# Mamba scan: three of sixteen inflows per chunk as TensorE products, every odd C product on GpSimd; last experts: the first two Silu built from Exp and Ln

## The chip, the cores and the metric

The kernel runs on one NeuronCore of a Trainium2 chip. The metric is the device time of one execution in microseconds. A core has TensorE (PE, matrix products into PSUM), VectorE (DVE), ScalarE (ACT), GpSimd (POOL) and SyncE (SP, which issues the transfers here). They run side by side, each through its own list of instructions in order, and wait for one another on semaphores.

## The reference, cut to what matters

Eight layers of a network over 2048 tokens with 128 channels, each `x = x + layernorm(layer(layernorm(x)))`. The change touches the last two.

```python
# layer 6, Mamba: 256 inner channels d, 16 states n
dA = jnp.exp(d_i[..., None] * A)                          # decay
h  = dA * h + (d_i * u_i)[..., None] * B_i[:, None, :]    # inflow: (delta*x) times B of the token
y  = jnp.einsum('bdn,bn->bd', h, C_i)
# layer 7, mixture of experts
h1 = jnp.einsum('td,eid->tei', xf, w1); h3 = jnp.einsum('td,eid->tei', xf, w3)
h  = jax.nn.silu(h1) * h3
y  = jnp.einsum('tei,edi,te->td', h, w2, comb)
```

## The kernel before

The sequence is cut into CHUNKS = 4 chunks of N = 512 tokens. Channels lie on the 128 partitions, in two halves i = 0, 1; tokens run along the free axis. The scan is 64 steps, one for each chunk c and state n (step = 16c + n). A step is made of these pieces:

- **Decays.** ScalarE writes exp(A·delta), one 128x512 half at a time, into one of three PSUM banks that take turns (`state_step`, `decays`).
- **Inflow.** GpSimd multiplies delta·x (`g[:, 6:8]`, both halves, 128x1024) by the row B_n, which SyncE has loaded into all partitions from DRAM (`b_times_du`, `b_copy`; four places, four steps ahead).
- **Scan.** VectorE runs two `tensor_tensor_scan`, one for each half (`scan`), into one of four state buffers: `g` for steps 0 and 1 of four, `y` for 2 and 3.
- **C product.** The states times the row C_n. VectorE reads the row from the one PSUM bank C_BANK (`times_c`), where TensorE has spread it over the partitions (`spread_c`, the `g,sel` product). For the steps in `BY_POOL` GpSimd does it with a row loaded from DRAM (`states_times_c`). The result lies in `tmp` or `rstd`.
- **Sum over n.** TensorE adds the products to PSUM banks 0 and 1 with an identity (`sum_n`, two 128x512 products; these are the `tmp,const` and `rstd,const` rows). Every float32 product shows as two matmul records in the trace, a bfloat16 one as one.

At n = 3 of the next chunk VectorE multiplies the two finished banks by the gate (`gate`, the row `g<-ps,g` 128x1024). Until that is done `sum_n` of the next chunk's first step may not start, since it clears the same banks. Then TensorE makes the output product (`out_of`, the `g,arena` rows), and the norms around layer 7 follow at n = 6, 8, 10, 12 and 14 (`post6_...`, `pre7_...`, `add_back6`, `h_back7`, `router7`).

All orders are written out by hand: each engine has a loop over the steps with `if`s for what is put between them. On VectorE the loop at k holds the extras of n = k mod 16, then `scan(k + 1)`, then `times_c(k)` unless k is in BY_POOL. On TensorE the loop at `step` holds `sum_n(step - 3)` for a step of GpSimd, `sum_n(step - 2)` for one of VectorE, the extras, and `spread_c(step + 1)` if that step is VectorE's.

After the scan come layer 7's turns, in each of which one pair of experts meets one chunk (`gate_up7`, `silu`, `glu7`, `hidden_hi`, `down7`). Routing for the first two chunks (`group_scores7`, `group_order7`, `kept7`, `chosen7`) is done on VectorE meanwhile. ScalarE has one table set for Exp and Ln and another for Silu, and loads a table when the set changes.

Of the kernel before, what the change touches and what calls it, by code (L numbers as in the profile page):

```python
# [29 lines left out]
P = 128  # L30
T = 2048
N = 512
# [66 lines left out]
BY_POOL = [s for s in range(STEPS) if s % 16 in (1, 3, 6, 8, 11, 13)]  # L99
# [147 lines left out]
def sandwich(nc, x, out, weights, bools, moe0, moe1, consts, selectors, rope):  # L247
    ctx = ExitStack()
    with ctx:
        def sb(name, shape, dt=F32):  # L250
# [12 lines left out]
            hid_ready e_done rows_stored row_loaded0 row_loaded1 a_ready xs_bank xs_ready conv_ready  # L263
            xa_ready z_bank z_ready dt_bank dt_ready dl_ready du_ready bc_bank bc_step dt_clipped bcp_ready b_copied
            cb_bank da_ready db_ready hs_done hc_ready hc_pool c_loaded0 c_loaded1 sum_done carry_saved
# [164 lines left out]
        def decays(step, i):  # L430

            return ps[:, DA_BANKS[(2 * step + i) % 3], :]
# [4 lines left out]
        def b_copy(step):  # L437
            home = arena[0][:, 1792:3840] if step < 48 else g[:, 8, :]
            return home[:, step % 4 * N:(step % 4 + 1) * N]
# [17 lines left out]
        def by_dve(step):  # L457
            return step + 1 - by_pool(step)

# [4 lines left out]
        def _(sp):  # L464
# [6 lines left out]
            for layer in range(LAYERS):  # L471
# [29 lines left out]
                if layer == 6:  # L501
# [14 lines left out]
                    for step in range(STEPS):  # L516
                        k = step % 4
# [7 lines left out]
                        if step == 48:  # L525
                            sp.wait_ge(s["dl_ready"], 2 * CHUNKS)
                        if step >= 4:
                            sp.wait_ge(s["db_ready"], step - 3)
                        sp.dma_start(b_copy(step), bc_dram[step % 16:step % 16 + 1, cols(step // 16)].to_broadcast([P, N]))\
                          .then_inc(s[f"row_loaded{k}"], 16)  # L530
                        if step - 7 in BY_POOL[:-2]:
                            load_c(by_pool(step - 7) + 1)
                if layer == 7:
# [6 lines left out]
                    for half in range(2):  # L540
# [4 lines left out]
                        for r in range(1, 9):  # L545
                            use = 8 * half + r - 1
                            if use < 4:
                                sp.wait_ge(s[f"row_loaded{use}"], ROWS_BEFORE[use] + 256)
# [79 lines left out]
        def _(pe):  # L628
# [594 lines left out]
            def xs(c):  # L1223
                h(6, c)
                for i in range(2):
                    mm(ps[:, 4 * i + c, :], W(6, "wx", i * 128, i * 128 + 128), H(c)).then_inc(s["xs_bank"], 1)
# [13 lines left out]
            for c in range(CHUNKS):  # L1240
                pe.wait_ge(s["xs_ready"], 2 * c + 2)
                for i in range(2):
                    mm(ps[:, 4 * i + c, :], W(6, "wz", i * 128, i * 128 + 128), H(c)).then_inc(s["z_bank"], 1)
            for c in range(CHUNKS):
                pe.wait_ge(s["z_ready"], 2 * c + 2)
                pe.wait_ge(s["xa_ready"], 2 * c + 2)
# [2136 lines left out]
```

## Time and profile before

| | us |
|---|---|
| median of 3 runs | 1102.28 (1101.16 to 1107.06) |
| the profiled execution, its time | 1102.07 |
| its span in the trace | 1100.1 |
| scan, from its first to its last step | 767.8 to 983 |
| busy over the span: TensorE / VectorE / GpSimd / ScalarE | 932.5 / 822.2 / 679.1 / 602.8 |

The time is 2.0 us more than the span. Busy shares of the span mix stages with different limits, so what matters for this change is read from the stretch of the scan and the 30 us after it. PE rows are products, PEld rows weight loads. `x4` after a row is the number of records in it. The bracket at its end is how long the engine had been idle and what it had waited for. Records of one engine can overlap by some 0.1 us at their ends, so the pace of a series is the distance from start to start.

### The profile page before, as it was taken

How to read it: one execution, taken by the hardware profiler on the slowest of the kernel's cores; microseconds unless marked ns; L12 is line 12 of the kernel's file. 1: busy time of each engine (PE TensorE's matmuls, PEld its weight loads, DVE VectorE, ACT ScalarE, POOL GpSimd, SP SyncE). 2: the span in 40 equal slices, each digit the busy share in tenths (PEclk: the TensorE clock that was granted, in tenths of full speed). 3: DMA queues.
4: the chain of work that ended last, by engine and by line, in shares of the span. 5: the costliest groups of instructions: out<-in, count | busy, mean ns of one | idle time of the engine just before them, and what ended most of it. 6: DMA issues, size and time to landing. Idle time of an engine off the chain costs nothing.

```text
span 1100.1 us, 11087 instructions
## 1 busy us (share of the span) xinstructions
PE 932.5 (85%) x2909; PEld 547.9 (50%) x2909; DVE 822.2 (75%) x1163; ACT 602.8 (55%) x1095; POOL 679.1 (62%) x469
## 2 busy tenths in 40 slices
PE   6869976688889957899999999987577787887997
PEld 3324432233337725688888888732223333335775
DVE  4895437999965568666666666587999999986755
ACT  5756675300356754455565555686444545545556
POOL 3030134699852133577777777619999999962773
PEclk9989998699999968899999999998788988897999
DMA  2000120000020004377666667302334334424251
GB/s 82 1 0 1 50 77 18 0 0 1 0 71 1 11 19 101 94 157 152 138 151 153 148 141 156 90 0 76 106 108 113 113 103 114 106 72 105 70 145 39
DMA packets 33449, 84.68 MB, mean 77 GB/s; under 512 B 4352, under 2 KB 14208, under 8 KB 29216
## 3 DMA queue, kind: packets, MB, share of 16 engines
q1 hardware_dynamic: 33408, 84.20, 30.5%
q8 instruction: 17, 0.28, 0.1%
q14 instruction: 24, 0.20, 0.1%
HBM read 82.22 MB, written 1.97 MB: 77 GB/s over the span
## 4 chain that ended last, share of the span: by engine, by line
PE 36%; DVE 16%; ACT 3%; issue 3%; POOL 1%; DVEq 0%; ACTq 0%; POOLq 0%
PE ps L630 35%; DVE y L3167 5%; DVE g L3167 5%; DVE tmp L2468 1%; DVE g L2468 1%; DVE rstd L2468 1%; ACT rstd L1440 1%; DVE ps L2468 1%; POOL g L2424 1%; ACT g L1440 1%; ACT ps L1440 1%; DVE normed L2468 0%; ACT sq L1440 0%; ACT parts L1440 0%; DVE g L3123 0%
## 5 line engine op out<-in xcount | busy, mean ns | idle before, releaser
L630 PE MATMUL ps<-parts 128*128 128x512 f32 x1704 | 416.5, 403 | 17.5 <-DVE g L2468 6.2
L630 PEld LDWEIGHTS ps<-parts 128*128 128x128 f32 x1704 | 321.6, 190 | 107.1 <-issue 18.3
L630 PE MATMUL ps<-g,arena 128*128 128x512 f32 (+2 forms) x408 | 191.2, 608 | 26.6 <-POOL g L2351 15.1
L1440 ACT ACTIVATE g<-ps 128x512 f32<-128x512 f32 (+1 forms) x216 | 127.3, 596 | 147.5 <-PE ps L630 143.1
L2302 POOL TENSOR_TENSOR parts<-g,parts 128x512 fp32r<-128x512 f32 x112 | 144.4, 1290 | 60.8 <-ACT parts L1440 57.9
L2468 DVE TENSOR_TENSOR ps<-g,ps 128x512 f32<-128x512 f32 x160 | 111.3, 695 | 94.5 <-PE ps L630 72.8
L1440 ACT ACTIVATE ps<-g,small 128x512 f32<-128x512 f32 x131 | 89.8, 688 | 98.3 <-DVE y L3167 52.9
L630 PEld LDWEIGHTS ps<-g,arena 128*128 128x128 f32 (+1 forms) x408 | 76.9, 197 | 133.1 <-issue 88.9
L1440 ACT ACTIVATE parts<-g 128x512 fp32r<-128x512 f32 (+3 forms) x243 | 125.9, 547 | 24.7 <-DVE g L2468 17.6
L2424 POOL TENSOR_TENSOR g<-g,arena 128x1024 f32<-128x1024 f32 x48 | 113.7, 2396 | 0.1
L2468 DVE TENSOR_TENSOR g<-ps,g 128x512 f32<-128x512 f32 (+1 forms) x140 | 98.9, 706 | 18.1 <-DVE ps L2468 3.3
L2292 POOL TENSOR_TENSOR parts<-g,parts 128x512 fp32r<-128x512 f32 x56 | 72.4, 1295 | 64.0 <-ACT parts L1440 63.8
L630 PE MATMUL ps<-normed,arena 128*128 128x512 f32 x136 | 76.0, 667 | 21.2 <-DVE g L2468 8.2
L2351 POOL TENSOR_TENSOR g<-g 128x1024 f32<-128x1024 f32 x32 | 76.2, 2391 | 19.5 <-DVE g L2826 18.5
L630 PE MATMUL ps<-tmp,const 128*128 128x512 f32 x128 | 73.3, 709 | 9.6 <-DVE g L2468 9.6
L3167 DVE TENSOR_TENSOR_SCAN g<-ps,carry,g 128x512 f32<-128x512 f32 x64 | 77.6, 1260 | 0.9 <-ACT ps L1440 0.9
L3167 DVE TENSOR_TENSOR_SCAN y<-ps,carry,g 128x512 f32<-128x512 f32 x64 | 77.8, 1261 | 0.0
L2826 DVE TENSOR_TENSOR_SCAN g<-ps,g 128x512 f32<-128x512 f32 x64 | 76.7, 1245 | 0.0
L1440 ACT ACTIVATE rstd<-ps,small 128x512 f32<-128x512 f32 x68 | 46.6, 685 | 38.5 <-PE ps L630 38.2
L630 PE MATMUL ps<-rstd,const 128*128 128x512 f32 x128 | 65.3, 640 | 0.0
L1440 ACT ACTIVATE sq<-ps 128x512 f32<-128x512 f32 x28 | 16.5, 593 | 87.8 <-PE ps L630 87.8
L630 PE MATMUL ps<-sq,const 128*128 128x512 f32 x96 | 52.5, 636 | 8.1 <-ACT sq L1440 5.9
(226 smaller groups left out, 1182.2 us busy)
## 6 DMA issues: line engine op xcount, KB each, us to landing
g<-coef_scratch SPq DMA_DIRECT2D x56, 512.0 KB, 6.2
arena<-bc_scratch SPq DMA_DIRECT2D x48, 256.0 KB, 3.3
g<-in_moe_dram SPq DMA_DIRECT2D x34, 192.0 KB, 4.7
g<-coef_scratch SPq DMA_DIRECT2D x24, 256.0 KB, 5.5
sq<-bc_scratch SPq DMA_DIRECT2D x24, 256.0 KB, 3.3
arena<-coef_scratch SPq DMA_DIRECT2D x24, 256.0 KB, 4.3
g<-bc_scratch SPq DMA_DIRECT2D x16, 256.0 KB, 3.3
g<-in_rope_dram SPq DMA_DIRECT2D x1, 2048.0 KB, 8.7
```

Source lines behind the costliest of these rows:

```text
L630: return nc.tensor.matmul(o, lhsT, rhs, start=start, stop=stop, **kw)
L1440: return nc.scalar.activation(o, i, func, **kw)
L2292: pv.tensor_tensor(hid_lo[:, cols(n % 4)], hidden, hid_hi[:, cols(n % 4)].bitcast(F32), ALU.subtract).then_inc(s["hl_ready"], 1)
L2302: pv.tensor_tensor(hid_lo[:, cols(c)], g[:, 6, (c % 2) * N:(c % 2 + 1) * N], hid_hi[:, cols(c)].bitcast(F32), ALU.subtract).then_inc(s["hl ...
L2351: pv.tensor_tensor(g[:, 2, 2 * par * N:(2 * par + 2) * N].rearrange("p (r n) -> p r n", r=2), fast_states(e), g[:, 8:10, cols(c)], ALU.mul ...
L2424: pv.tensor_tensor(inflow(step), g[:, 6:8, cols(step // 16)], b_copy(step).unsqueeze(1).to_broadcast([P, 2, N]), ALU.mult).then_inc(s["db_ ...
L2468: return v.tensor_tensor(o, a, b, op)
L2826: last = v.tensor_tensor_scan(state, fast_decay(c), two_of(0, 11, k)[:, r, :], state[:, N - 1:N] if c else 0.0, ALU.mult, ALU.add)
L3167: ins = v.tensor_tensor_scan(states(step % 4)[:, i, :], decays(step, i), inflow(step)[:, i, :], carry[:, n + 16 * i:n + 16 * i + 1], ALU.m ...
```

## The change

Three things change.

1. In steps with n = 6, 10 and 14 (`BY_PE`, 12 of 64) the inflow is a TensorE product: delta·x turned so that tokens are on partitions (`du_turned`) times a 128x128 diagonal of B's values (`b_diag`), four 128x128 products for each half, into the PSUM bank that the decays had. The decays of these steps go to the SBUF place that the inflow had. For this TensorE turns B (`b_turned`) and delta·x (`du_into`, `du_turn`), and ScalarE copies what was turned (`du_copied`) and builds the diagonals (`diag_of_b`, four 128x128 instructions a step).
2. `BY_POOL` becomes every odd step but the last: 31 steps in place of 24.
3. In layer 7 the first two Silu are x·exp(-ln(1 + exp(-x))), with a clip and two multiplications on VectorE (`clip_gate7`, `glu7`) and three functions on ScalarE (`sigmoid_of`), so that they run before the Silu table is loaded. Turn 2's gate and up products, and both routing steps `kept7` and `chosen7`, move forward.

```diff
-BY_POOL = [s for s in range(STEPS) if s % 16 in (1, 3, 6, 8, 11, 13)]
+BY_POOL = [s for s in range(STEPS - 1) if s % 2 == 1]
+BY_PE = [s for s in range(STEPS) if s % 16 in (6, 10, 14)]
+B_ROWS = [s for s in range(STEPS) if s not in BY_PE]
...
         def decays(step, i):
-            return ps[:, DA_BANKS[(2 * step + i) % 3], :]
+            return inflow(step)[:, i, :] if step in BY_PE else flow_bank(step, i)
+        def flow(step, i):
+            return flow_bank(step, i) if step in BY_PE else inflow(step)[:, i, :]
...
+            def b_turned():
+                for c in range(CHUNKS):
+                    for a in range(TILES):
+                        at = 256 + (c * TILES + a) * 16
+                        last = mm(ps[:, 0, at:at + 16], bc_whole[:, c * N + a * P:c * N + (a + 1) * P], ident[0:96, 0:16])
+                last.then_inc(s["dut_bank"], 1)
+            def du_into(bank, c, half):
+                for a in (2 * half, 2 * half + 1):
+                    for i in range(2):
+                        at = (a % 2 * 2 + i) * P
+                        last = nc.tensor.transpose(ps[:, bank, at:at + P], g[:, 6 + i, c * N + a * P:c * N + (a + 1) * P],
+                                                   ident)
+                last.then_inc(s["dut_bank"], 1)
...
+            def inflow_by_pe(step):
+                c = step // 16
+                pe.wait_ge(s["x_parts"], diag_parts(step))
+                for i in range(2):
+                    pe.wait_ge(s["hs_done"], 2 * step + i - 2)
+                    for a in range(TILES):
+                        last = mm(flow(step, i)[:, a * P:(a + 1) * P], du_turned(c, a, i),
+                                  b_diag(step)[:, a * P:(a + 1) * P])
+                    last.then_inc(s["x_bank"], 1)
...
             spread_c(0)
+            b_turned()
+            pe.wait_ge(s["du_ready"], 1)
+            du_into(4, 0, 0)
+            du_into(7, 0, 1)
...
             for step in range(STEPS):
                 c, n = step // 16 - 1, step % 16
+                if step + 1 in BY_PE:
+                    inflow_by_pe(step + 1)
                 if step - 3 in BY_POOL:
                     sum_n(step - 3)
...
+                if c < 2 and n in (11, 15):
+                    du_turn(c + 2, n // 15)
                 if step + 1 < STEPS and step + 1 not in BY_POOL:
                     spread_c(step + 1)
...
-            pre7_var(3)
             coef_turned7(0)
             coef_turned7(1)
+            pre7_var(3)
+            gate_up7(2)
             router7(3)
...
             for step in range(STEPS):
                 c, n = step // 16 - 1, step % 16
                 state_step(step)
                 if step == 1:
+                    act.wait_ge(s["dut_bank"], 1)
+                    f(b_by_token, ps[:, 0, 256:512], ACT.Copy).then_inc(s["x_parts"], 1)
+                    du_copied(0, 0)
+                    du_copied(0, 1)
...
                 if step >= 2:
                     save_carry(step - 2)
+                if step + 3 in BY_PE:
+                    diag_of_b(step + 3)
...
+            sigmoid_of(0)
             post6_square(3)
             post6_root(3)
-            pre7_square(3)
-            pre7_root(3)
+            sigmoid_of(1)
             coef_copied7(0)
             coef_copied7(1)
+            pre7_square(3)
+            hidden_hi(0)
+            pre7_root(3)
             sigmoid7(1)
...
-                        if step + 4 < STEPS:
+                        if step + 4 in B_ROWS:
                             b_times_du(step + 4)
...
             h_back7(2)
+            group_scores7(0)
             gate(CHUNKS - 1)
+            clip_gate7(0)
+            group_order7(0)
             clip7(2)
-            group_scores7(0)
-            group_order7(0)
             kept7(0)
+            chosen7(0)
+            clip_gate7(1)
+            glu7(0)
             add_back6(3)
-            chosen7(0)
+            glu7(1)
             h_back7(3)
```

**TensorE's list after a gate.** These are the instructions from `spread_c(18)` on in the program before, up to the second C row that is spread after the gate; the product that waits for `yg_ready` is `sum_n(16)`, the first behind the gate.

```order
L630 MATMUL ps<-g,sel 128x512 [waits hc_ready]
L630 MATMUL ps<-tmp,const 128x512 [waits hc_ready,yg_ready]
L630 MATMUL ps<-tmp,const 128x512
L630 MATMUL ps<-g,arena 128x512 [waits yg_ready]
L630 MATMUL ps<-g,arena 128x512
L630 MATMUL ps<-g,sel 128x512 [waits hc_ready]
L630 MATMUL ps<-tmp,const 128x512 [waits hc_pool]
L630 MATMUL ps<-tmp,const 128x512
L630 MATMUL ps<-rstd,const 128x512 [waits hc_ready]
L630 MATMUL ps<-rstd,const 128x512
L630 MATMUL ps<-g,sel 128x512 [waits hc_ready]
```

The same place in the changed program, from `sum_n(15)` on.

```order
L663 MATMUL ps<-rstd,const 128x512 [waits hc_pool]
L663 MATMUL ps<-rstd,const 128x512
L663 MATMUL ps<-tmp,const 128x512 [waits hc_ready,yg_ready]
L663 MATMUL ps<-tmp,const 128x512
L663 MATMUL ps<-g,arena 128x512 [waits x_parts,yg_ready]
L663 MATMUL ps<-g,arena 128x512
L663 MATMUL ps<-g,sel 128x512 [waits hc_ready]
L663 MATMUL ps<-tmp,const 128x512 [waits hc_pool]
L663 MATMUL ps<-tmp,const 128x512
L663 MATMUL ps<-rstd,const 128x512 [waits hc_ready]
L663 MATMUL ps<-rstd,const 128x512
L663 MATMUL ps<-arena,g 128x128 [waits hs_done,x_parts]
```

The row `arena,g` is the first of the eight products of step 22's inflow. It stands behind `sum_n(16)`, `out_of(0)`, `spread_c(20)`, `sum_n(17)` and `sum_n(18)`.

**ScalarE's list at the start of the scan.** The rows `ps<-g,small` are the decays; those that follow the copies belong to step 2. Before:

```order
L1440 ACTIVATE ps<-g,small 128x512 [waits hs_done]
L1440 ACTIVATE arena<-ps 128x256 [waits setup_bank]
L1440 ACTIVATE ps<-g,small 128x512 [waits hs_done] x2
L1440 ACTIVATE carry<-g 128x2 [waits hs_done]
```

In the changed program:

```order
L1521 ACTIVATE ps<-g,small 128x512 [waits hs_done]
L1521 ACTIVATE arena<-ps 128x256 [waits dut_bank]
L1521 ACTIVATE g<-ps 128x512 [waits dut_bank] x2
L1521 ACTIVATE arena<-ps 128x256 [waits setup_bank]
L1521 ACTIVATE ps<-g,small 128x512 [waits hs_done] x2
L1521 ACTIVATE carry<-g 128x2 [waits hs_done]
```

Three copies that wait for TensorE (`dut_bank`: B turned, then the two halves of delta·x turned) now stand ahead of step 2's decays.

## Rows read from the trace of the kernel before

**Rows 1.** Windows: length, busy (count) PE, PEld, DVE, ACT, POOL; clock; DMA; GB/s.
```profile
767.80:983.00 215.20, 161.64 (x346) 67.86 (x345) 210.98 (x183) 107.51 (x216) 208.50 (x91) 0.86 0.39 108
```

**Rows 2.** Groups of instructions on VectorE, 767.8 to 983: busy, mean ns, idle before.
```profile
L2468 DVE TENSOR_TENSOR tmp<-g,ps 128x1024 f32<-128x1024 f32 x20 | 23.9, 1197 | 3.1 <-PE ps L630 2.9
```

**Rows 3.** Groups of instructions on GpSimd, 767.8 to 983.
```profile
L2424 POOL TENSOR_TENSOR g<-g,arena 128x1024 f32<-128x1024 f32 x47 | 111.4, 2397 | 0.0
...
L2434 POOL TENSOR_TENSOR tmp<-g,sq 128x1024 f32<-128x1024 f32 x12 | 29.2, 2437 | 3.0 <-PE ps L630 2.0 <-DVE g L3167 1.0
```

**Rows 4.** Waits, 767.8 to 983: total, times, longest.
```profile
DVE tmp L2468 <- PE ps L630: 2.9, 2, 1.9
...
DVE rstd L2468 <- PE ps L630: 0.6, 1, 0.6
```

**Rows 5.** Timeline at the first gate: VectorE, then TensorE.
```profile
834.42 1.19 DVE L2468 TENSOR_TENSOR rstd<-y,ps 128x1024 f32<-128x1024 f32 x1
835.53 1.21 DVE L2468 TENSOR_TENSOR g<-ps,g 128x1024 f32<-128x1024 f32 x1
836.67 4.79 DVE L3167 TENSOR_TENSOR_SCAN g<-ps,carry,g 128x512 f32<-128x512 f32 x4
843.39 1.22 DVE L2468 TENSOR_TENSOR tmp<-g,ps 128x1024 f32<-128x1024 f32 x1 [1.94 <-PE ps L630]
...
836.80 3.78 PE L630 MATMUL ps<-tmp,const 128*128 128x512 f32 x4 [4.61 <-DVE g L2468]
840.37 2.77 PE L630 MATMUL ps<-g,arena 128*128 128x512 f32 x4
842.97 0.38 PE L630 MATMUL ps<-g,sel 96*128 96x512 bf16 x1
```

**Rows 6.** Timeline of TensorE at the second gate, which ends at 891.74.
```profile
891.79 1.98 PE L630 MATMUL ps<-tmp,const 128*128 128x512 f32 x4 [2.45 <-DVE g L2468]
893.61 1.88 PE L630 MATMUL ps<-g,arena 128*128 128x512 f32 x4
895.33 0.38 PE L630 MATMUL ps<-g,sel 96*128 96x512 bf16 x1
```

**Rows 7.** Timeline of TensorE at the third gate, which ends at 943.83.
```profile
943.89 3.18 PE L630 MATMUL ps<-tmp,const 128*128 128x512 f32 x4 [2.55 <-DVE g L2468]
...
949.12 0.38 PE L630 MATMUL ps<-g,sel 96*128 96x512 bf16 x1
```

**Rows 8.** A window of 4 us, TensorE only: length, busy (count), clock, DMA, GB/s.
```profile
836.00:840.00 4.00, 3.20 (x4) 0.50 0.49 118
```

**Rows 9.** Timeline at the start of the scan.
```profile
767.03 1.22 PE L630 MATMUL ps<-const,arena 128*128 128x128 f32 x4 [6.67 <-DVE g L3139]
...
771.50 0.69 ACT L1440 ACTIVATE ps<-g,small 128x512 f32<-128x512 f32 x1 [0.48 <-DVE g L3167]
...
773.67 2.45 DVE L3167 TENSOR_TENSOR_SCAN y<-ps,carry,g 128x512 f32<-128x512 f32 x2
```

**Rows 10.** Timeline of TensorE: small products, first a router, then transposes.
```profile
989.97 0.96 PE L630 MATMUL ps<-arena,normed 128*128 128x16 f32 x8
...
1092.59 1.04 PE L1430 MATMUL ps<-const,normed 128*128 128x128 f32 x8
```

**Rows 11.** Timeline behind the scan.
```profile
990.96 0.23 DVE L3057 TENSOR_SCALAR g<-ps 128x64 f32<-128x64 f32 x1 [2.87 <-PE ps L630]
...
994.54 0.70 DVE L2468 TENSOR_TENSOR ps<-ps,sq 128x512 f32<-128x512 f32 x1
...
997.35 0.29 DVE L3098 SCALAR_TENSOR_TENSOR arena<-arena,g 128x128 f32<-128x128 f32 x1
...
1000.88 1.89 PE L630 MATMUL ps<-arena,normed 128*128 128x16 f32 x8 [0.42 <-DVE normed L2468]
...
1004.17 1.28 ACT L1440 ACT_TABLE_LOAD   x1
...
1009.31 0.70 DVE L2468 TENSOR_TENSOR ps<-g,ps 128x512 f32<-128x512 f32 x1 [1.40 <-PE ps L630]
```

More of the change, by code:

```diff
@@ L458, in by_dve, with by_pe, of_rows, turned_parts @@
             return step + 1 - by_pool(step)
+        def by_pe(step):
+            return sum(k <= step for k in BY_PE)
+        def of_rows(step):
+            return step + 1 - by_pe(step)
+        def turned_parts(c, part):
+            return 1 + part if c == 0 else 3 + 5 * (c - 1) + 3 + part
+        def diag_parts(step):
+            return 3 + 5 * (step // 16) + BY_PE.index(step) % 3 + 1
         block = ctx.enter_context(nc.Block())
@@ L524, in _ @@
                             sp.wait_ge(s["rows_stored"], 96)
[L525 to L532, printed above, removed]
+                        if step not in BY_PE:
+                            use = of_rows(step) - 1
+                            if use >= 4:
+                                sp.wait_ge(s["db_ready"], use - 3)
+                            sp.dma_start(b_copy(use), bc_dram[step % 16:step % 16 + 1, cols(step // 16)]
+                                         .to_broadcast([P, N])).then_inc(s[f"row_loaded{use % 4}"], 16)
+                        if step - 6 in BY_POOL[:-2]:
+                            load_c(by_pool(step - 6) + 1)
                 if layer == 7:
@@ L2025, in state_step, with du_copied, diag_of_b @@
                       scale=neg_a[:, n + 16 * i:n + 16 * i + 1]).then_inc(s["da_ready"], 1)
+            def du_copied(c, half):
+                act.wait_ge(s["dut_bank"], 2 * c + half + 2)
+                at = c % 2 * 1024 + half * N
+                f(g[:, 8, at:at + N], ps[:, 7 if (c, half) == (0, 1) else 4, :], ACT.Copy).then_inc(s["x_parts"], 1)
+            def diag_of_b(step):
+                act.wait_ge(s["x_parts"], 1)
+                if by_pe(step) > 2:
+                    act.wait_ge(s["x_bank"], 2 * (by_pe(step) - 2))
+                for a in range(TILES):
+                    at = (step // 16 * TILES + a) * 16 + step % 16
+                    last = f(b_diag(step)[:, a * P:(a + 1) * P], ident, ACT.Copy, scale=b_by_token[:, at:at + 1])
+                last.then_inc(s["x_parts"], 1)
             def save_carry(step):
@@ L3159, in scan @@
                 n = step % 16
-                dve.wait_ge(s["db_ready"], step + 1)
+                if step not in BY_PE:
+                    dve.wait_ge(s["db_ready"], of_rows(step))
                 if step >= 4:
```

104 lines of the change are left out of this document (72 added, 32 removed).

## The prediction

> **What bounds the kernel now.** I read the windows first, since only the scan and the start of layer 7 change. In the scan's 215.2 us VectorE is busy for 211.0 and GpSimd for 208.5, TensorE for 162 and ScalarE for 108 [rows 1]. So VectorE sets the end of the scan with 4.2 us of idle time, GpSimd is close behind, and both have to shrink for the scan to. The groups give the price of what moves: a C product takes VectorE 1.20 us [rows 2] and GpSimd 2.44, and an inflow takes GpSimd 2.40 [rows 3]. VectorE's idle time is mostly waiting for TensorE [rows 4]: 1.9 and 1.0 us ahead of C products into `tmp` and 0.6 ahead of one into `rstd`. The longest is behind a gate: the C product at 843.39 came 1.94 us late [rows 5].
>
> **How a gate works.** The gate ends at 836.74. The four scans behind it take from 836.67 to 841.46 [rows 5], so I count 2.4 us for the two scans of a step, and 1.11 us for a C product (834.42 to 835.53). TensorE had been idle for 4.61 us, because `sum_n(16)` may not clear the banks before the gate has read them, and restarted at 1.2 GHz: its granted clock from 836 to 840 was 0.50 [rows 5, 8]. The sum took 3.57 us from start to start, `out_of` 2.60, and the next C row came at 842.97, 6.2 us behind the gate. At the second gate TensorE had been idle for 2.45 us and went on at twice that pace, 2.4 GHz: 1.82 us for the sum, 1.72 for `out_of`, and the C row 3.6 us behind the gate [rows 6]. At the third, after 2.55 us idle, the sum took most of 3.18 us and the C row came 5.3 us behind the gate [rows 7].
>
> **What is taken away.** Seven C products leave VectorE: 7 x 1.11 = 7.8 us. GpSimd loses 12 inflows and gains 7 C products, 5 fewer of about 2.4 us, so 12 us less. A chunk of 16 steps then costs VectorE 16 x 2.4 + 8 x 1.11 = 47.3 us and the extras (gate, add-back and norm, some 3.5), GpSimd 13 + 8 = 21 instructions or 50.4 us. VectorE with its 50.8 stays ahead by a hair, and a wait of VectorE's behind each gate gives GpSimd room. I take all 7.8; the bound below is GpSimd in front, which would eat up to 2.
>
> **What a TensorE inflow costs.** No row shows this product. The nearest are 128x128 transposes, 8 in 1.04 us or 0.12 apiece, and products of 16 columns, 8 records in 0.96 us, also 0.12 [rows 10], so the weight load of one seems to lie under the product of the other. A float32 product is two records. A step is 8 products, 16 records; at 0.11 us, half a step (4 products) is 0.86 us and the step 1.75. The other bound is load and product one after the other, twice that. I take the low one, as both rows are at it. The Trainium skill, TensorE: Matmul & The Clock Gate, Back-to-back issue gap, gives about 81 ns for each pass of 128 columns in a sustained stream with weight loads. By an estimate with four passes for a float32 product half a step would be 1.3 us, and the three gates together 1.3 us dearer than by the rows.
>
> **In the middle of a chunk** the rows say that it fits. Two steps of VectorE are 4 x 1.2 + 1.11 = 5.9 us. TensorE's work between the C product that lets it go on and the first half of an inflow is one C row (0.22), two sums (3.44) and 0.86, and with 0.15 of latency 4.7 us: 1.2 us early. At 1.2 GHz the same list is 0.43 + 7.1 + 1.72 + 0.15 = 9.4 us, 3.5 late. In chunk 0 VectorE's three long products (`g<-g`, 128x1024) leave TensorE idle between bursts, so I put 1.0 us on steps 6 and 10 together.
>
> **Behind a gate** it does not fit. The order shows that step 22's inflow stands behind `sum_n(16)`, which waits for the gate, then `out_of(0)`, `spread_c(20)`, `sum_n(17)` and `sum_n(18)`. VectorE wants it two steps and a C product behind the gate, at 5.9 us. At the full clock TensorE has 4 x 1.72 + 0.22 + 0.86 + 0.2 = 8.2: 2.3 us late. With the C row 6.2 us behind, as at the first gate, it is 6.2 + 0.22 + 3.44 + 0.86 + 0.15 = 10.9, or 5.0 late; with the third gate's 5.3, 4.1 late [rows 5 to 7]. Which clock? In the changed kernel `sum_n(15)` is done 1.95 us behind the C product of step 16, and the gate ends 7.1 behind it (four scans 4.8, a C product 1.1, the gate 1.2). TensorE is then idle for 5.2 us, longer than at the first gate, which came out at 1.2 GHz; of two waits of about 2.5 us one did. So I take 4.2 us a gate, near the two at 1.2 GHz: 12.6 for three, with 7 and 15 as ends. The waits for TensorE before (2.9 and 0.6, in all 3.5 [rows 4]; the timeline has all three within 8 us of a gate) are contained in it and come off.
>
> The Trainium skill, TensorE: Matmul & The Clock Gate, HAM oscillation, warns that repeated waits between bursts put the array back to half rate each time. By that rule all three gates would be at 1.2 GHz, at 13 to 15 us; one of three at the full clock is what this trace has against it.
>
> **At the start.** Step 2's decays were issued at 771.50, and its scan at 773.67 [rows 9]. Now three ScalarE copies stand ahead of them and wait for TensorE: 16 products that turn B (32 records) and 8 transposes. TensorE is free for them at about 768.5 (the group from 767.03 and one C row). At 0.12 us the records take 3.8, at 1.2 GHz 0.236 (the router at 1000.88, 1.89 for 8 [rows 11]) 7.6. I take a third of them at 1.2 GHz, 5.3 us, so 773.8; the transposes end at 774.7, the last copy at 775.4, the output weights' copy 775.8, the decays 776.5, and the scan starts at 776.55: 2.9 us late. Ends: 1.4 and 6.2. The later copies and diagonals lie in ScalarE's idle half; if that cover is gone, a diagonal group is 4 instructions of 0.3 to 0.4 us ahead of the next decays, which have 1.7 us to spare.
>
> **Behind the scan.** The path before: add-back at 994.54, router 1000.88, table load 1004.17, turn 2 on VectorE at 1009.31 [rows 11]. A VectorE product of 128x512 takes 0.70, so the add-back's two end at 995.94, and `chosen7` behind them takes the 1.7 us to 997.64. After the change a clip (0.7), `chosen7` and turn 0 (1.4) stand ahead of the add-back together with routing that was there before. VectorE's wait of 2.87 us for the router of chunk 2 is filled with the other clip and the routing's first part (1.9 in all), which leaves kept7 at 991.2. From there 1.6 + 1.7 + 0.7 + 1.4 put the add-back at 996.6, 2.1 late. The router of chunk 3, 6.3 us behind the add-back before, may start at 1002.9. It may also wait for turn 2's six products, which are put ahead of it. Router (1.0 or 1.9), clip and sigmoid (1.4), a weight copy (0.5), the table load (1.28) and turn 2's Silu (0.6): turn 2 starts on VectorE between 1007.6 and 1008.8. It had started at 1009.31, so 0.5 to 1.7 less; I take 1.1. Turns 0 and 1 are hidden in the routing's wait.
>
> **The sum** is made against the profiled execution's 1102.07, which is within 0.3 us of the median 1102.28: 1102.1 - 7.8 (C products) - 3.5 (the gates' old waits) + 12.6 (the gates' new ones) + 1.0 (chunk 0) + 2.9 (start) - 1.1 (turns) = **1106.2**, say 1106.
>
> **Rivals.**
> - *TensorE keeps the full clock.* The gates cost 2.3 each (6.9), the start 1.4 and chunk 0 nothing: 1102.1 - 7.8 - 3.5 + 6.9 + 1.4 - 1.1 = 1098. The second gate speaks for it [rows 6], and TensorE has about 20 us more to do, which keeps it awake; against it stands the 5.2 us of idling. Chance 0.22.
> - *No new wait behind the gates*, since the inflow comes in time by some slack I don't see (the sums faster, VectorE slower there). Only the start remains: 1102.1 - 7.8 - 3.5 + 2.9 - 1.1 = 1092.6. The list speaks against it: 1.72 four times alone is 6.9, over the 5.9. Chance 0.14.
> - *TensorE becomes the bound away from the gates too* (the slower side). The nine other inflows have 1.2 us to spare at the full clock and are 3.5 late at the lower. It decides as soon as TensorE has idled long enough ahead of one; in chunks 0 to 2 it idles for up to 3 us between bursts. Four of the nine at 1.2 GHz add 14, less the 1.0 that is counted: 1119. If instead load and product do not overlap, the gates cost 2.6 more and it is 1109. Together 0.16.
> - The forecast as it stands, 1101 to 1111: 0.48.
>
> **Range and chances.** 1092 to 1113 holds all but the far part of the third rival and the edge of the second; the forecast's own range is 1101 to 1111. A change under 0.5% (5.5 us) can't be told from none. Below 1096.8 lie the case without waits and a fifth of the full-clock one: 0.22. Above 1107.8 lie the third rival and a quarter of the forecast: 0.28. The rest, 0.50, is within 0.5%.
>
> **What the changed profile would show.** VectorE idle before a scan `y<-g,carry,ps` of steps 22, 38 and 54, released by TensorE, 2 to 5 us each; TensorE idle for about 5 us ahead of each gate; GpSimd with 52 inflows and 31 C products; VectorE's C products 33; step 2's scan about 3 us late with ScalarE's copies ahead of it; inflow products at 0.11 us a record; turn 2 near 1008. I am wrong if the scans behind the gates start on time, if waits show at steps 10 and 14 of a chunk, or if VectorE waits for GpSimd (`hc_pool` or `db_ready`) at all.

## The result: 1114.06 us, one per cent slower

The changed kernel takes 1114.06 us (median of 4 runs, 1113.91 to 1116.89) against 1103.32 before (4 runs beside it, 1101.16 to 1107.06): a recorded ratio of 1.009, 95% interval 1.0072 to 1.0108 (the plain quotient of the two medians is 1.0097). The forecast was 1106, in a range that ended at 1113. Its profiled execution took 1114.01, with a span of 1112.2.

The window answers to [rows 1], same length, columns as there:

```profile
767.80:983.00 215.20, 174.60 (x558) 92.11 (x559) 193.33 (x170) 118.37 (x263) 189.82 (x84) 0.86 0.43 97
```

VectorE's load fell, but it idles for 22 of the 215 us where it idled for 4. The view of waits (the changed kernel, 767.8 to 998: total, times, longest) says for whom, and answers to [rows 4]:

```profile
DVE y L3289 <- PE ps L663: 11.6, 5, 3.2
DVE y L3289 <- ACT ps L1521: 4.9, 1, 4.9
DVE tmp L2587 <- PE ps L663: 4.3, 3, 1.5
DVE g L3289 <- ACT ps L1521: 1.8, 2, 1.0
DVE rstd L2587 <- PE ps L663: 0.9, 1, 0.9
```

Nothing of GpSimd is in the list. Its groups from 767.8 to 998, in answer to [rows 3], have the 52 inflows and 31 C products of the forecast, at 2.36 us:

```profile
L2543 POOL TENSOR_TENSOR g<-g,arena 128x1024 f32<-128x1024 f32 x52 | 121.8, 2361 | 0.1
L2553 POOL TENSOR_TENSOR tmp<-g,sq 128x1024 f32<-128x1024 f32 x16 | 37.7, 2355 | 4.8 <-DVE g L3289 2.7 <-PE ps L663 2.0
L2553 POOL TENSOR_TENSOR rstd<-y,sq 128x1024 f32<-128x1024 f32 x15 | 35.4, 2359 | 22.7 <-DVE y L3289 19.3 <-PE ps L663 3.5
```

**The first gate**, timeline of VectorE and then of TensorE in the changed kernel, in answer to [rows 5]:

```profile
842.50 1.22 DVE L2587 TENSOR_TENSOR g<-ps,g 128x1024 f32<-128x1024 f32 x1
843.63 4.80 DVE L3289 TENSOR_TENSOR_SCAN g<-ps,carry,g 128x512 f32<-128x512 f32 x4
849.90 1.22 DVE L2587 TENSOR_TENSOR tmp<-g,ps 128x1024 f32<-128x1024 f32 x1 [1.47 <-PE ps L663]
854.32 2.45 DVE L3289 TENSOR_TENSOR_SCAN y<-g,carry,ps 128x512 f32<-128x512 f32 x2 [3.20 <-PE ps L663]
...
843.77 3.78 PE L663 MATMUL ps<-tmp,const 128*128 128x512 f32 x4 [4.01 <-DVE g L2587]
847.34 2.30 PE L663 MATMUL ps<-g,arena 128*128 128x512 f32 x4
849.48 0.38 PE L663 MATMUL ps<-g,sel 96*128 96x512 bf16 x1
849.70 1.88 PE L663 MATMUL ps<-tmp,const 128*128 128x512 f32 x4
851.41 1.88 PE L663 MATMUL ps<-rstd,const 128*128 128x512 f32 x4
853.13 1.95 PE L663 MATMUL ps<-arena,g 128*128 128x128 f32 x16
```

This is the list of the prediction. After 4.01 us of idling the sum takes 3.57 us from start to start, and the granted clock from 843 to 847 is 0.50, which is 1.2 GHz. Part of the output product is faster already (granted clock 0.85 from 847 to 851), and the C row stands 5.8 us behind the gate. Two sums of 1.72 and the first half of the inflow follow at 2.4 GHz. VectorE waits first for the C row, then for the inflow. The other two gates are the same to 0.1 us (1.43 and 3.20, 1.41 and 3.20), 13.9 in all. The first of the two waits depends on the execution: numbers 1 and 4 below, with the same list at the gates, have 0.96 to 1.40 there, and 3.20 each time for the inflow.

**The start**, ScalarE, TensorE and VectorE, in answer to [rows 9]:

```profile
778.09 0.39 ACT L1521 ACTIVATE arena<-ps 128x256 f32<-128x256 f32 x1 [5.51 <-PE ps L663]
...
771.20 6.85 PE L663 MATMUL ps<-const,arena 96*128 96x16 f32 x32
777.89 1.95 PE L1312 MATMUL ps<-const,g 128*128 128x128 f32 x8
...
781.43 2.46 DVE L3289 TENSOR_TENSOR_SCAN y<-ps,carry,g 128x512 f32<-128x512 f32 x2 [4.95 <-ACT ps L1521]
```

The 32 records that turn B take 6.85 us, 0.21 each. The window around them has a granted clock of 0.50, so all of it ran at 1.2 GHz:

```profile
770.50:785.00 14.50, 13.36 (x49) 10.11 (x47) 9.49 (x8) 7.85 (x18) 13.79 (x6) 0.50 0.24 76
```

The kernel before has the same clock at this place. A window of it, TensorE only (length, busy, clock, DMA, GB/s):

```profile
774.00:776.00 2.00, 2.00 (x4) 0.50 0.32 86
```

**Behind the scan** VectorE's turn 2 starts at 1020.24, 22.9 us behind the end of the last C product; before it was 24.7 (1009.31 [rows 11] against 984.65).

### The profile page after: what moved, and what is told of

It is laid out like the page before. It is cut to its first block, busy times and chain, and to the rows that moved or that the text cites. A ratio compares the mean times of both kernels' runs of the same rounds, so it can differ in the third digit from the quotient of the medians.

```text
span 1112.2 us, 11662 instructions
## 1 busy us (share of the span) xinstructions
PE 958.4 (86%) x3158; PEld 577.8 (52%) x3158; DVE 817.6 (74%) x1160; ACT 620.8 (56%) x1156; POOL 665.6 (60%) x464
## 4 chain that ended last, share of the span: by engine, by line
PE 39%; DVE 12%; ACT 3%; issue 3%; POOL 1%; DMA 1%; DVEq 0%; SPq 0%; ACTq 0%; POOLq 0%
PE ps L663 38%; DVE y L3289 4%; DVE g L3289 3%; DVE g L2587 1%; DVE tmp L2587 1%; ACT g L1521 1%; ACT rstd L1521 1%; DVE rstd L2587 1%; DVE ps L2587 1%; DMA g<-in_moe_dram 1%; ACT ps L1521 1%; POOL parts L2410 0%; POOL tmp L2553 0%; ACT sq L1521 0%; DVE normed L2587 0%
## 5 line engine op out<-in xcount | busy, mean ns | idle before, releaser
L1521 ACT ACTIVATE g<-ps 128x512 f32<-128x512 f32 (+1 forms) x222 | 131.0, 596 | 149.3 <-PE ps L663 142.4
L2543 POOL TENSOR_TENSOR g<-g,arena 128x1024 f32<-128x1024 f32 x52 | 121.8, 2361 | 0.1
L1521 ACT ACTIVATE ps<-g,small 128x512 f32<-128x512 f32 x107 | 72.0, 685 | 78.0 <-DVE y L3289 46.7
L663 PE MATMUL ps<-tmp,const 128*128 128x512 f32 x128 | 70.5, 680 | 11.8 <-DVE g L2587 11.8
L663 PEld LDWEIGHTS ps<-normed,arena 128*128 128x128 f32 x136 | 27.6, 210 | 60.9 <-issue 44.9
```

Source lines behind the costliest of these rows:

```text
L663: return nc.tensor.matmul(o, lhsT, rhs, start=start, stop=stop, **kw)
L1521: return nc.scalar.activation(o, i, func, **kw)
L2543: pv.tensor_tensor(inflow(step), g[:, 6:8, cols(step // 16)], b_copy(use).unsqueeze(1).to_broadcast([P, 2, N]), ALU.mult).then_inc(s["db_r ...
```

## The experiments

Each was timed against the kernel before on the same chip (medians there 1104.51 for the first four, then 1103.15, then 1103.69). The ratios are the recorded ones; they can differ by 0.001 from the quotient of the medians. "Scan" is from the start of the first scan to the end of the last C product, "behind" from there to the end of the span, both from the profiled execution.

| kernel | median us | ratio to before | 95% | scan | behind |
|---|---|---|---|---|---|
| before | 1103.32 | 1 | | 216.8 | 115.5 |
| changed | 1114.06 | 1.0090 | 1.0072 to 1.0108 | 226.8 | 114.9 |
| 1 copies later | 1109.67 | 1.0055 | 1.0036 to 1.0073 | 221.4 | 114.8 |
| 2 inflow first | 1108.99 | 1.0041 | 1.0028 to 1.0054 | 222.7 | 114.8 |
| 3 TensorE kept busy | 1107.01 | 1.0031 | 1.0017 to 1.0045 | 220.7 | 115.2 |
| 4 scan only | 1114.31 | 1.0073 | 1.0044 to 1.0101 | 227.5 | 112.8 |
| 5 turns only | 1102.41 | 0.9986 | 0.9964 to 1.0007 | 216.6 | 115.0 |
| 6 two inflows | 1105.19 | 1.0022 | 0.9996 to 1.0049 | 219.2 | 115.5 |
| 7 GpSimd odd, no inflows | 1118.60 | 1.0133 | 1.0106 to 1.0160 | 232.8 | 114.1 |
| 8 two inflows, mended | 1102.40 | 0.9983 | 0.9966 to 1.0000 | 217.8 | 113.8 |
| 9 and weights earlier | 1096.53 | 0.9936 | 0.9916 to 0.9955 | 210.5 | 112.8 |
| 10 and third inflow at step 8 | 1094.85 | 0.9921 | 0.9899 to 0.9943 | 208.1 | 114.3 |
| 11 and the new turns | 1096.39 | 0.9926 | 0.9898 to 0.9953 | 209.0 | 114.8 |
| 12 changed, weights earlier | 1111.69 | 1.0077 | 1.0052 to 1.0101 | 225.7 | 115.6 |

**1. ScalarE's copies one step later.** They stand behind the decays of step 2 now.

```diff
                 state_step(step)
-                if step == 1:
+                if step == 2:
                     act.wait_ge(s["dut_bank"], 1)
                     f(b_by_token, ps[:, 0, 256:512], ACT.Copy).then_inc(s["x_parts"], 1)
```

> ScalarE's three start copies stand behind step 2's decays instead of ahead of them; nothing else differs from the changed kernel (1114). If the copies in ScalarE's list cause the 4.95 us ahead of step 2's scan, that wait goes to under 1 us and the time to 1109 to 1111. Rival: TensorE's turning of B and delta-x itself is what is late, so the wait only moves, to the C product of step 2 or to step 6's inflow, and the time stays at 1113 to 1115.

The wait of 4.95 us before step 2 is gone. One of 0.78 us before step 3 is left, and in chunk 0 step 10 waits 2.02 us where steps 6 and 10 had waited 1.37 and 0.59. The scan is 5.4 us shorter, and the median 4.4. So TensorE's slow turning of B costs 4.95 us only because ScalarE's copies stand ahead of step 2's decays; one step later it costs little.

**2. The gate's inflow ahead of the two sums.** Step 22's inflow (and 38's, 54's) is issued one step earlier in TensorE's order.

```diff
-                if step + 1 in BY_PE:
+                if step + 1 in BY_PE and not (step > 16 and (step + 1) % 16 == 6):
                     inflow_by_pe(step + 1)
+                if step > 16 and step % 16 == 4:
+                    inflow_by_pe(step + 2)
```

> Behind each gate the inflow products of n = 6 stand ahead of the sums of n = 1 and 2 in TensorE's list. If the place in the list is the cause, the 3.20 us ahead of the scans of steps 22, 38 and 54 go, the 1.4 us ahead of the C product at the gate stay, and the time is 1114 - 9.6 = 1104 to 1106. Rival: TensorE is simply full around the gates, so that the two sums pushed back make the next C row or inflow late by as much: 1111 to 1114.

VectorE behind the first gate of this kernel:

```profile
847.63 1.22 DVE L2589 TENSOR_TENSOR tmp<-g,ps 128x1024 f32<-128x1024 f32 x1 [0.99 <-PE ps L663]
848.77 2.44 DVE L3291 TENSOR_TENSOR_SCAN y<-g,carry,ps 128x512 f32<-128x512 f32 x2
...
858.74 0.70 DVE L2589 TENSOR_TENSOR ps<-ps,sq 128x512 f32<-128x512 f32 x1 [1.70 <-ACT sq L1523]
```

The three waits of 3.20 us are gone. In their place the add-back waits 1.70 us each time: the sums are later, the variance product behind them too, and ScalarE's root after it. Of 9.6 us, 5.1 are given back there, and the scan is 4.1 us shorter. The time, 1108.99, lies between the two that were expected: TensorE has a backlog behind a gate, and this order moves half of the cost to another wait.

**3. TensorE kept busy through the wait for the gate.** Four unread products stand ahead of the sum that waits.

```diff
+                if step > 16 and step % 16 == 2:
+                    if c:
+                        pe.wait_ge(s["sc_clipped"], 2 + c)
+                    for _ in range(4):
+                        mm(ps[:, 7, :], averaging, G(6, 0))
                 if step >= 2 and step - 2 not in BY_POOL:
                     sum_n(step - 2)
```

> Four products more, whose result nothing reads, stand between the sum of n = 15 and the first sum behind each gate, so that TensorE idles less than 2 us there; the output is unchanged. If the clock of 1.2 GHz behind the gate makes 4.7 us out of the 2.3 that the list alone costs, the granted clock behind the gates is 1.00, the wait ahead of the C product goes, the one ahead of the inflow falls to about 2.3, and the time is 1114 - 7 = 1106 to 1109. Rival: the clock does not follow these 3 us of work, the waits stay at 1.4 and 3.2, and the time at 1113 to 1115.

TensorE and VectorE at its first gate:

```profile
841.39 1.88 PE L663 MATMUL ps<-tmp,const 128*128 128x512 f32 x4
843.11 1.88 PE L663 MATMUL ps<-g,arena 128*128 128x512 f32 x4
844.83 0.38 PE L663 MATMUL ps<-g,sel 96*128 96x512 bf16 x1
...
849.67 2.45 DVE L3294 TENSOR_TENSOR_SCAN y<-g,carry,ps 128x512 f32<-128x512 f32 x2 [2.61 <-PE ps L663]
```

The sum takes 1.72 us instead of 3.57 (granted clock 1.00 from 840 to 852), the C row comes in time, and 2.61 us remain before the inflow. The prediction had 2.3 for a gate at the full clock. The scan is 6.1 us shorter, 2.0 a gate: that was the price of the clock, and the other 2.6 are TensorE's work.

**4. The changed scan with the old turns of layer 7.** The functions and the order behind the scan are those of before, for example

```diff
-            for n in range(2, len(TURNS7)):
-                if n > 2:
-                    gate_up7(n)
+            for n in range(2, len(TURNS7)):
+                gate_up7(n)
```

> The changed scan with the old first turns of layer 7 (Silu from its table, routing and turn 2 in their old places). The stretch behind the scan took 0.6 us less in the changed kernel than before, so this should take 0 to 1 us more than the changed kernel: 1114 to 1115. Rival: the changed turns lose time and the shorter stretch is the scan's doing; then this is 1112 or less.

The stretch behind the scan took 112.8 us, 2.1 less than with the new turns, as the rival had it; the median is that of the first expectation (1114.31 against 1114.06). The profiled execution, which is the median one, entered the scan 1.7 us later and took 0.7 more for it, so that the two readings do not contradict each other.

**5. The kernel before with the new turns.**

```diff
+            def clip_gate7(n):
+                dve.wait_ge(s["g_bank"], TURN7 + n + 1)
+                v.tensor_scalar(silu7(n), ps[:, 4 if n == 0 else 7, :], -80.0, None, ALU.max).then_inc(s["dt_clipped"], 1)
```

and the rest of the turns' edits as in the change. The clip is the first of the instructions from which the two Silu are built.

> The kernel before with one thing changed: the new first two turns of layer 7 (Silu from Exp and Ln, and the order around them); the scan is the old one. Theory 1, the prediction's term: the turns give 1.1 us back, 1103.4 against 1104.5 before. Theory 2, from the run with the scan alone changed (the stretch behind the scan took 112.8 us with the old turns and 114.85 with the new): the new turns cost 2 us wherever they stand, 1106.5. Theory 3: with the old scan the stretch behind it is one at 1.2 GHz in either order (three groups of small products at 1.9 to 2.1 us), so the turns make no difference, 1104.5 within 0.5. The trace is to tell 2 from 3: in 2 the second turn's first glu on VectorE stands 2 us later behind the scan than in the kernel before (24.7 us), in 3 it stands where it was.

0.9986, with 1 inside the interval: at most 4 us gained and at most 0.8 lost. Turn 2 starts 23.0 us behind the last C product (24.7 before), and yet the whole stretch shrinks by 0.5 only. Turn 2 is neither 2 us later (second theory) nor where it was (third). That does not show a gain by the turns either: in number 4, with the old turns, it starts at 22.9 too. The section on the prediction comes back to this.

**6. Two inflows a chunk on TensorE**, at steps 10 and 14; step 6's goes back to GpSimd. The two counters of copies (`turned_parts`, `diag_parts`) follow.

```diff
-BY_PE = [s for s in range(STEPS) if s % 16 in (6, 10, 14)]
+BY_PE = [s for s in range(STEPS) if s % 16 in (10, 14)]
```

> The changed kernel with two inflows a chunk on TensorE (steps 10 and 14) in place of three; step 6's goes back to GpSimd. Theory A (the waits at the gates are TensorE's backlog, and the inflow of step 6 is the last thing in it): the three waits of 3.20 us go, the waits of 1.4 us ahead of the C product stay, and chunk 0's step 6 loses its 1.4: 1114.1 - 9.6 - 1.4 = 1103, a scan of about 216. GpSimd has 4 instructions more, 87 at 2.36 = 205 us, and does not bind. Theory B (what leaves TensorE is given back elsewhere, as in the run with the inflow issued earlier): the add-back of each chunk waits 1.7 us instead, 1108. Theory C (GpSimd is already close to the bound, as a product with C at odd steps stands in a row with inflows): VectorE waits for GpSimd in every chunk, over 1112.

The 3.20s and chunk 0's 1.37 are gone, GpSimd holds nothing up, and the C products wait 2.14, 1.70 and 1.48. But a new wait stands near the end, on VectorE:

```profile
971.99 2.46 DVE L3289 TENSOR_TENSOR_SCAN g<-ps,carry,g 128x512 f32<-128x512 f32 x2 [3.94 <-ACT ps L1521]
985.16 1.22 DVE L2587 TENSOR_TENSOR rstd<-y,ps 128x1024 f32<-128x1024 f32 x1 [3.77 <-PE ps L663]
```

In the changed kernel the first was 0.98 and the second 0.89. Number 9 is on it.

**7. The kernel before with the C products of all odd steps on GpSimd** and no inflow on TensorE.

```diff
-BY_POOL = [s for s in range(STEPS) if s % 16 in (1, 3, 6, 8, 11, 13)]
+BY_POOL = [s for s in range(STEPS - 1) if s % 2 == 1]
...
-                        if step - 7 in BY_POOL[:-2]:
-                            load_c(by_pool(step - 7) + 1)
+                        if step - 6 in BY_POOL[:-2]:
+                            load_c(by_pool(step - 6) + 1)
```

The second part moves the loads of C's rows on SP along with the steps; the changed kernel has it too.

> The kernel before with one thing changed: the C products of all odd steps on GpSimd (31 in place of 24), all 64 inflows still there; nothing of the inflows on TensorE, the old layer 7 turns. Theory A: GpSimd becomes the bound, 95 instructions at 2.36 us make 224 us, with two smaller ones of layer 7 about 226, where the scan took 216.8: 1111 to 1114, VectorE's waits ended by GpSimd in every chunk, those at the gates absorbed. Theory B: there is slack enough between the engines, VectorE keeps its pace and saves seven products at 1.11 us: 1096 to 1098.

GpSimd is busy for 224.4 of the 232.8 us, and one of VectorE's waits reads

```profile
890.12 2.46 DVE L3167 TENSOR_TENSOR_SCAN y<-ps,carry,g 128x512 f32<-128x512 f32 x2 [0.99 <-POOL g L2424]
```

and so on at every second step for most of the later chunks. Theory A's 224 us for 95 instructions is right, and there are 6.5 us of the new wait near the end on top: it comes with the C products at the odd steps and not with TensorE's inflows. Without inflows taken off GpSimd, the seven C products lose 1.3%.

**8. Two inflows, and the edits of 1, 3 and 4 with them.** The diff shows neither the counters, which are as in 6, nor the old turns, as in 4.

```diff
-BY_PE = [s for s in range(STEPS) if s % 16 in (6, 10, 14)]
+BY_PE = [s for s in range(STEPS) if s % 16 in (10, 14)]
...
-                if step == 1:
+                if step == 2:
...
+                if step > 16 and step % 16 == 2:
...
+                    for _ in range(4):
+                        mm(ps[:, 7, :], averaging, G(6, 0))
```

> The changed kernel with four edits: two inflows a chunk on TensorE instead of three, ScalarE's start-up copies one step later, four unread products ahead of each gate on TensorE that keep its clock up, and the old turns of layer 7. Theory A (the terms of the account add up): 1114.1 - 9.6 - 1.4 (third inflow) - 4.2 (C product's waits at the gates) - 3 (start) - 2 (turns) = 1094, faster than the kernel before by 1 per cent: VectorE waits for TensorE nowhere for more than 1 us from step 3 to the last gate. Theory B (they do not: the unread products delay the sums, or GpSimd binds once VectorE is fast): 1100 or above, with waits of VectorE ended by GpSimd, since 87 instructions at 2.36 us = 205 us come near a scan of 211.

1102.40, not 1094. From step 3 to step 60 VectorE waits for TensorE once, 0.60 us. GpSimd now binds three times (1.03, 1.10 and 1.00 us), and the wait near the end has grown to 5.59, with 3.48 behind it. ScalarE and SP there:

```profile
964.34 0.60 ACT L1522 ACTIVATE ps<-sq 128x512 f32<-128x512 f32 x1
970.53 0.52 ACT L1522 ACTIVATE parts<-g 128x384 fp32r<-128x384 f32 x1 [5.59 <-DMA g<-in_moe_dram]
...
956.86 0.43 SPq L562 DMA_DIRECT2D arena<-bc_scratch  x1
963.45 0.32 SPq L545 DMA_DIRECT2D sq<-bc_scratch  x1
963.87 0.39 SPq L569 DMA_DIRECT2D g<-in_moe_dram  x1
```

ScalarE's `weights7_hi(0)` waits for layer 7's weights ahead of the decays that the scan wants. They are issued on SP behind the last row of C (`sq<-bc_scratch`), which waits until the C product of two before is done on GpSimd. The transfer itself takes 7 us. With C products at the odd steps that product is step 57's, before the change step 56's: the order of the change moved the weights one step toward their reader. GpSimd adds to it: it waits for VectorE ahead of its C products in the changed kernel (2.83 us before the one at 968.54), while here it is busy without a break up to 970.3, so that the product which frees the row is later against VectorE. How the 5.59 us divide between the two was not measured.

**9. The weights ahead of the last row of C**, and the rest as in 8. The two loads are taken out of their place behind the loop; their operands are not shown.

```diff
                     for step in range(STEPS):
+                        if step == STEPS - 1:
+                            sp.wait_ge(s["centred"], CHUNKS * 7 + 3)
+                            sp.dma_start(g[:, 3, 0:4 * PAIR]...
+                            sp.dma_start(g[:, 2, 0:4 * PAIR]...
                         if step - 6 in BY_POOL[:-2]:
                             load_c(by_pool(step - 6) + 1)
```

> The kernel of the last run (two inflows a chunk, copies later, unread products at the gates, old turns) with layer 7's first two weight loads issued on SP's queue behind the row of B of step 63 and ahead of the last row of C, where they stood behind it. Theory A: the scan's wait of 5.59 us for ScalarE at step 61 is the wait for this transfer, which was issued 6.6 us after the last row of B because the last row of C waits for its buffer; the wait goes, and with it most of the 3.48 and 1.62 us in which VectorE then waited for TensorE, which had gone idle meanwhile: 1102.4 - 5.6 - 2.6 = 1094. Theory B: the weights (2 x 768 KB) then stand in the way of the last row of C, GpSimd's last product comes late, and 3 us or more of the gain go: 1097 to 1100.

```profile
958.53 0.43 SPq L562 DMA_DIRECT2D arena<-bc_scratch  x1
959.00 0.43 SPq L566 DMA_DIRECT2D g<-in_moe_dram  x1
...
968.69 2.46 DVE L3290 TENSOR_TENSOR_SCAN g<-ps,carry,g 128x512 f32<-128x512 f32 x2 [0.85 <-ACT ps L1523]
978.98 1.22 DVE L2588 TENSOR_TENSOR rstd<-y,ps 128x1024 f32<-128x1024 f32 x1 [0.89 <-PE ps L664]
```

The wait falls from 5.59 to 0.85 and the one behind it from 3.48 to 0.89: 7.3 us of scan. The second came with the first: in number 8 TensorE idled 4.52 us meanwhile, and the sum behind it took 3.45 us in place of 1.88 (granted clock 0.50 from 974 to 978).

**10. The third inflow back on TensorE, at step 8**, with number 9's other edits and the counters for three.

```diff
-BY_PE = [s for s in range(STEPS) if s % 16 in (10, 14)]
+BY_PE = [s for s in range(STEPS) if s % 16 in (8, 10, 14)]
```

> As the run before it in this list, with three inflows a chunk on TensorE again, at steps 8, 10 and 14 of a chunk instead of 6, 10 and 14. Theory A: what a third inflow costs is its place behind the gate, not its number: no wait of 3.2 or 2.6 us at the gates, the three waits for GpSimd of 1.0 to 1.1 us are gone since GpSimd has 4 instructions fewer (83), so 3 us under the run before it: 1091. Theory B: TensorE and ScalarE (12 more operations for the four diagonal blocks) have no room for a third inflow wherever it stands: VectorE waits for them at steps 8 to 10 or at the add-back, 1095 or above.

In each chunk behind a gate one wait is left, before step 8's own inflow:

```profile
844.03 1.18 DVE L2588 TENSOR_TENSOR rstd<-y,ps 128x1024 f32<-128x1024 f32 x1
846.50 2.45 DVE L3290 TENSOR_TENSOR_SCAN g<-g,carry,ps 128x512 f32<-128x512 f32 x2 [1.29 <-PE ps L664]
```

Three times 1.29 us, where step 6 cost 2.61 a gate at the same clock, and no wait for GpSimd, which had made 2.6 us in number 9. The scan is 2.5 us shorter than in 9. Both theories have a part: at step 8 the third inflow costs half of what it costs at step 6, and step 8 is still in the backlog. The medians, 1094.85 and 1096.53, have overlapping intervals.

**11. The same with the new turns of layer 7**, for example

```diff
-            for n in range(2, len(TURNS7)):
-                gate_up7(n)
+            for n in range(2, len(TURNS7)):
+                if n > 2:
+                    gate_up7(n)
```

> As the run before it in this list, with the new first turns of layer 7 instead of the old ones. Theory A (the stretch behind the scan took 112.8 to 114.1 us with the old turns where the scan was changed, and 114.8 to 115.5 with the new ones): 1 to 2 us slower than with the old turns. Theory B (the old turns' stretch is the one that varies with TensorE's clock at its start, 115.45 in the kernel before): the two agree within 0.5 us.

1096.39, 1.5 us over number 10, and the stretch behind the scan 0.5 longer. The intervals overlap, so which turns are better is not shown by the times.

**12. The changed kernel with the weights earlier**, that edit alone.

```diff
+                        if step == STEPS - 1:
+                            sp.wait_ge(s["centred"], CHUNKS * 7 + 3)
```

with the two loads behind it, as in 9.

> The changed kernel with one edit: the two weight loads of layer 7 issued ahead of the last row of C, as in the first run of this list. Theory A: in the changed kernel the scan's wait of 0.98 us for ScalarE at step 61 goes, and no more, since the scan is late there by its own waits: 1113. Theory B: the wait is only replaced by one for GpSimd or TensorE: 1114, the same.

The wait of 0.98 us is gone and the scan is 1.1 us shorter. The median is 2.4 us lower, but 2.4 us is also what this profiled execution entered the scan earlier. In the changed kernel the late weights cost one microsecond, because VectorE was late by its other waits. They cost 7 in number 8, where it was not.

## Why the prediction came out too low

In the profiled executions the scan takes 226.8 us after 216.8, the stretch behind it 0.6 less, and the scan starts 2.7 us later (770.57 after 767.84). The terms, as predicted and as measured:

| term | predicted | measured |
|---|---|---|
| seven C products | -7.8 | -7.8 (pace as predicted) |
| the gates' old waits | -3.5 | -3.5 |
| the gates' new waits | +12.6 | +13.9 |
| chunk 0, steps 6 and 10 | +1.0 | +2.0 (1.37, 0.59; in number 2, with the same code there, 3.2) |
| start | +2.9 | +4.95 |
| ScalarE at step 61, for the weights | none | +1.0 |
| turns of layer 7 | -1.1 | -0.6 for the whole stretch, not shown to be the turns' |
| ahead of the scan | none | +2.7 in this execution |

The measured terms without the last row make 10.0, the medians differ by 10.7. The sum missed 1114.06 by 7.9 us: 5.8 of it lie in the terms, 1.2 in the base (1102.1, where the median beside the changed kernel is 1103.32), and 0.9 in no term, which is less than executions of one kernel differ by.

**The mechanism at the gates was right.** The inflow of step 22 waits behind `sum_n(16)`, `out_of(0)`, `spread_c(20)` and the two sums; TensorE idles ahead of it and restarts at 1.2 GHz; steps 10 and 14 fit in chunks 1 to 3; GpSimd holds up nothing; an inflow step is 16 records in 1.95 us with the last one's latency, 1.8 from start to start or 0.11 a record. TensorE idled 3.9 to 4.0 us there, not 5.2, since `sum_n(15)` itself took 2.8 us at the second and third gate and not 1.95. Number 3 shows the split by taking the clock's part away. The Trainium skill, TensorE: Matmul & The Clock Gate, HAM oscillation, describes a return to half rate after every wait between bursts, which means three slow gates. This trace agrees: the granted clock behind each of the three was 0.50, and the waits make 13.9 us, inside the 13 to 15 worked out for that case; I had leaned on one fast gate of before and took 12.6. The Trainium skill, TensorE: Matmul & The Clock Gate, Back-to-back issue gap, has 81 ns a pass, from which the estimate for half a step was 1.3 us. This trace does not agree: it is 0.9.

**The step that failed** is the clock taken for the start, "I take a third of them at 1.2 GHz, 5.3 us". All 32 records and the transposes ran at 1.2 GHz, which, with ScalarE's copies ahead of step 2's decays, puts that step's scan 4.95 us late and not 2.9; the end of that term's bound (6.2) held it. (A third of them slow makes 5.1 us by the sum's own figures, not 5.3.) The trace of before could have told: TensorE had idled 6.67 us [rows 9], and its granted clock was still 0.50 from 774 to 776. The same error stands behind chunk 0, where TensorE idles 4.09 and 3.66 us ahead of the bursts with steps 6 and 10 and restarts at 1.2 GHz: a C row takes 0.61 us there, 0.38 at the full clock. It was put at 1.0 us and measured 2.0.

**The step that was missing** is SP's queue. The change moves the C products to odd steps, hence the last row of C, hence the weight load behind it, and I didn't follow it. It cost 1.0 here (number 12), and 7.3 once the other waits were gone (8 against 9).

**The turns.** Turn 2 started 1.8 us earlier behind the scan, against 0.5 to 1.7 predicted, but this is TensorE's clock and not shown to be the turns. In the profiled execution of before three small groups of products ahead of turn 2 ran at 1.2 GHz, the last of them the router [rows 11]:

```profile
996.68 2.08 PE L630 MATMUL ps<-sq,const 128*128 128x512 f32 x2 [3.33 <-ACT sq L1440]
998.54 1.92 PE L1328 MATMUL ps<-const,arena 128*16 128x128 f32 x8
```

In number 4, which has the same old turns, they ran at 2.4 GHz:

```profile
1011.75 1.12 PE L663 MATMUL ps<-sq,const 128*128 128x512 f32 x2 [3.35 <-ACT sq L1517]
1012.77 1.04 PE L1401 MATMUL ps<-const,arena 128*16 128x128 f32 x8
1015.01 1.06 PE L663 MATMUL ps<-arena,normed 128*128 128x16 f32 x8 [1.20 <-DVE normed L2582]
```

There turn 2 starts 22.9 us behind the last C product, as in the changed kernel, and the stretch takes 112.8 us. With the old turns the stretch took 112.8 to 115.5 us, with the new ones 114.8 to 115.6. In the changed kernel six records of turn 2 stand ahead of the router of chunk 3, as the prediction feared:

```profile
1012.16 3.48 PE L663 MATMUL ps<-parts 128*128 128x512 f32 x6
1015.48 0.96 PE L663 MATMUL ps<-arena,normed 128*128 128x16 f32 x8
```

The router starts 18.1 us behind the last C product, in number 4 15.3. So the gain of 1.1 us is not shown, and the traces lean to a loss.

The shortfalls are 2.0 (start), 1.3 (gates), 1.0 (chunk 0), 1.0 (weights) and 0.5 (turns). In the traces the first three have one cause, TensorE at 1.2 GHz behind waits of 3.7 to 6.7 us, so they come out at the same end together; an experiment took the clock's part away at the gates only. I had taken a middle for each. One more slip: the chance below 1096.8 is 0.14 and a fifth of 0.22, 0.18 and not 0.22.

## What to carry to other kernels

Before work is moved to an engine that waits in bursts, list what stands ahead of it in that engine's order at the point where the consumer wants it, and cost the list at the clock that the engine has after its wait; terms that hang on the same clock are summed at the same end. When the consumers of a buffer move, follow every load in the DMA queue behind the one that waits for the buffer, to its reader. And a change that loses may only be placed badly: three inflows a chunk and 31 C products on GpSimd, with five edits (third inflow at step 8, copies later, unread products, weights earlier, old turns), run at 0.992 of the kernel before instead of 1.009. What the unread products alone would give the kernel before was not run; its waits at the gates are 3.5 us [rows 4], and the scan of number 10 is 8.7 us shorter than its scan, so they can't account for all of it.

## What the runs showed of the hardware

- The time at which the scan begins varied from 767.2 to 772.9 us over the profiled executions, although hardly any code ahead of it differs. Before and after differ by 2.7 us, with the same instructions. The difference arises between 65 and 90 us: the last GpSimd product `g<-g,y` of layer 0 begins at 65.2 and at 65.0, the first VectorE product `y<-g,tmp` at 90.2 and at 92.9. In between TensorE was granted the full clock later. Windows of 4 us there, TensorE first, the kernel before and then the changed one:

```profile
68.00:72.00 4.00, 4.00 (x11) 1.79 (x10) 3.35 (x11) 1.20 (x2) 0.00 (x0) 1.00 0.00 0
80.00:84.00 4.00, 4.00 (x10) 1.55 (x9) 3.96 (x6) 3.04 (x5) 1.34 (x1) 1.00 0.00 0
```

```profile
68.00:72.00 4.00, 4.00 (x8) 1.63 (x7) 2.23 (x4) 0.60 (x1) 0.00 (x0) 0.76 0.00 0
80.00:84.00 4.00, 4.00 (x6) 1.43 (x6) 3.71 (x6) 1.20 (x2) 1.47 (x1) 0.57 0.00 0
```

- A handful of products whose results nobody reads can pay: four of them ahead of each wait gave 2.0 us a gate back, and the sum behind them took 1.72 us in place of 3.57.
- A late transfer that held ScalarE for 5.6 us cost VectorE 4.7 us at once and 2.6 more later, as TensorE had idled and its next products ran at 1.2 GHz (number 8 against 9).
